# Attention slots taken two at a time, with the softmax denominators applied after the product with the values

## The reference

```python
q = heads(xn @ wq.T); lat = xn @ w_kv_down.T; k = heads(lat @ w_k_up.T); v = heads(lat @ w_v_up.T)   # 16 heads of 64
q, k = rope(q), rope(k)
probs = softmax(q @ k.T / 8 + causal)
s = (probs @ v, heads joined) @ wo.T
e_star = max(top-2 experts of xn @ gate_w + gate_b)
g = silu(2 * (gelu(xn @ w1[e_star] + b1[e_star]) @ w2[e_star] + b2[e_star]))
out = x + s * g
```

## Time and profile before

| | |
|---|---|
| median of 3 runs | 309.83 us (309.74 to 309.87) |
| the profiled execution | 310.5 us, span 308.7 us |
| PE / DVE / ACT / POOL busy | 294.3 / 221.0 / 242.9 / 215.9 us |
| granted TensorE clock | 0.998 |
| chain that ended last | PE 64%, POOL 12%, issue 11%, DVE 8%, ACT 2% |

### The profile page before, as it was taken

One profiled execution on the slowest core, in us unless ns is written; L12 is line 12 of the kernel. 1 busy time (PEld: TensorE's weight loads), 2 busy tenths in 40 slices (PEclk: granted clock), 3 DMA queues, 4 the chain that ended last, 5 costly groups with the idle time before them and its releaser, 6 DMA issues.

```text
span 308.7 us, 8487 instructions
## 1 busy us (share of the span) xinstructions
PE 294.3 (95%) x2362; PEld 235.4 (76%) x2362; DVE 221.0 (72%) x883; ACT 242.9 (79%) x851; POOL 215.9 (70%) x321
## 2 busy tenths in 40 slices
PE   8897999999999999999999989999989999899994
PEld 3566878888888888777777789999867777786763
DVE  3889998987787998988887523323278789898651
ACT  3387889898887889999897665555799999889982
POOL 3378878786786879999999933332138999889730
PEclk9999999999999999999999999999999999999999
DMA  6764595979333333333345470000063334344200
GB/s 204 232 140 112 107 308 124 225 168 302 74 69 71 68 71 89 92 87 87 99 104 134 129 197 0 2 2 0 3 187 71 93 102 115 103 108 133 71 19 17
DMA packets 39596, 33.35 MB, mean 108 GB/s; under 512 B 4801, under 2 KB 36674, under 8 KB 39554
## 3 DMA queue, kind: packets, MB, share of 16 engines
q1 hardware_dynamic: 38098, 30.51, 38.3%
q0 software_dynamic: 1024, 2.10, 2.5%
q10 hardware_dynamic: 432, 0.23, 0.3%
HBM read 11.07 MB, written 4.98 MB: 52 GB/s over the span
## 4 chain that ended last, share of the span: by engine, by line
PE 64%; POOL 12%; issue 11%; DVE 8%; ACT 2%; DMA 1%; POOLq 1%; SPq 0%; DVEq 0%; ACTq 0%
PE bank L1092 9%; PE bank L1080 8%; PE bank L1106 7%; PE bank L1120 6%; PE bank L1285 6%; PE bank L1300 6%; POOL probs L474 5%; POOL staged L463 4%; PE bank L1054 3%; DVE rot_out L585 3%; PE bank L1108 3%; PE bank L1082 3%; DVE masked L594 2%; PE bank L1188 2%; PE bank L1070 2%
## 5 line engine op out<-in xcount | busy, mean ns | idle before, releaser
L885 ACT ACTIVATE pexp<-masked,negmax 128x128 f32<-128x128 f32 (+1 forms) x256 | 114.1, 452 | 1.5 <-DVE negmax L594 1.4
L474 POOL TENSOR_SCALAR probs<-pexp,rden 128x256 f32<-128x256 f32 (+1 forms) x184 | 80.3, 451 | 26.0 <-DVE rden L601 23.3
L594 DVE CUSTOM_DVE_ANT_0 masked<-bank,mask 128x128 f32<-128x128 f32 (+1 forms) x256 | 75.9, 351 | 27.1 <-PE bank L1082 26.9
L463 POOL TENSOR_TENSOR staged<-rot_out 128x512 f32<-128x512 f32 x63 | 80.2, 1275 | 17.8 <-DVE rot_out L585 17.3
L585 DVE TENSOR_TENSOR rot_out<-bank,rot 128x1024 f32<-128x1024 f32 x64 | 77.6, 1214 | 4.0 <-PE bank L1056 2.7
L907 ACT COPY probsT<-bank 128x384 f32<-128x384 f32 x128 | 54.9, 480 | 22.9 <-PE bank L1092 21.9
L1092 PE MATMUL bank<-ident,probs 128*128 128x128 f32 x384 | 54.7, 275 | 1.8 <-ACT probsT L907 0.9
L885 ACT ACTIVATION_READ_ACCUMULATOR pexp<-masked,negmax 128x1 f32 x256 | 49.9, 195 | 0.0
L1080 PE MATMUL bank<-qk_sb 64*128 64x256 f32 x256 | 45.0, 427 | 2.9 <-DVE negmax L594 2.1
L1092 PEld LDWEIGHTS bank<-ident,probs 128*128 128x128 f32 x384 | 43.1, 140 | 5.2 <-POOL probs L474 1.9
L1120 PE MATMUL bank<-vo_sb,ctxT 128*128 128x128 f32 x256 | 39.4, 278 | 0.7 <-ACT ctxT L914 0.7
(11 more groups left out here) (113 smaller groups left out, 458.1 us busy)
## 6 DMA issues: line engine op xcount, KB each, us to landing
qk_sb<-staged SPq DMA_DIRECT2D x128, 128.0 KB, 2.5
w_sb<-in_w SPq DMA_DIRECT2D x2, 1024.0 KB, 5.6
w_sb<-in_w SPq DMA_DIRECT2D x4, 512.0 KB, 4.9
sorted_x<-z SPq DMA_DIRECT2D x1, 1408.0 KB, 7.9
sorted_g<-z SPq DMA_DIRECT2D x1, 1152.0 KB, 5.5
out<-res SPq DMA_DIRECT2D x8, 128.0 KB, 1.8
x_sb<-in_x SPq DMA_DIRECT2D x3, 256.0 KB, 3.8
rot<-in_c_rot SPq DMA_DIRECT2D x1, 512.0 KB, 5.0
```

What stands on the lines that cost most here:

```text
L463: pool.tensor_tensor(staged[:, n % 2, :, m % 2, :], rot_out[:, m % 2, :, 0:S], rot_out[:, m % 2, :, S:2 * S], op=ALU.add).then_inc(staged_ ...
L474: pool.tensor_scalar(probs[:, g % 2, i, c], pexp[:, g % 2, i, c], rden[:, g % 2, i, k:k + 1], 1.0, ALU.mult, ALU.mult).then_inc(probs_read ...
L594: t = dve.tensor_tensor_reduce(masked[:, g % 2, i, c], s_bank[i][:, c], mask[:, c], -1.0, -NEG * 1e8, ALU.add, ALU.min, negmax[:, g % 2, i ...
L885: e = act.activation(pexp[:, g % 2, i, c], masked[:, g % 2, i, c], ACT.Exp, bias=negmax[:, g % 2, i, k:k + 1], scale=-1.0, accum_out=rowsu ...
```

## The change

From slot 24 on (`FIRST_DOUBLE`) each engine takes two slots at a time (`couple(g)`, g even). The exponentials are transposed as they are, without `scale`. The eight reciprocals of a token row (two slots, two heads, two row halves) are transposed by PE to eight rows, copied by ACT to `rden_rows`, written to DRAM by one transfer and read back by two that spread them over 64 partitions each (`shares`); `ctx_out`, now on DVE, multiplies the result of `values` by them. Only slots 38, 39, 62 and 63 are still scaled first, by DVE and POOL, in place. `scores_of_two` puts the rests of two slots side by side in `s_bank` and their corners in `t_bank`; DVE must have read the corners before `turn` may write there. PE's order in a couple is: scores of the next two slots, outputs g-4 and g-3, a projection, `turn(g)`, a projection, `turn(g+1)`, values of g-2 and g-1. `TWICE` moves from (36, 38) to (23, 25). No slot from 24 on stands in `ALONE`.

```diff
-TWICE = (36, 38)
+TWICE = (23, 25)
...
-ALONE = tuple(range(FIRST_DOUBLE)) + (G_LEAD - 2, G_LEAD - 1, B * NP - 2, B * NP - 1)
+ALONE = tuple(range(FIRST_DOUBLE))
...
+def coupled(g):
+    return g >= FIRST_DOUBLE
...
+def scaled(g):
+    return g < FIRST_DOUBLE or g in (G_LEAD - 2, G_LEAD - 1, LAST, LAST + 1)
...
+def units(u):
+    return [n for n in range(UNIT, u + 1) if not scaled(2 * n)]
...
-        rden = sb("rden", [P, 2, 2, 2])
+        rden = sb("rden", [P, 2, 2, 2, 2])
...
+        def corner(g, i):
+            if g % 4 < 2 or not coupled(g - 2):
+                return masked[:, g % 2, i, 0:P]
+            return more_corners[:, g % 2, i, :]
...
+        def v_bank(g):
+            return s_bank[1] if g == G_LEAD - 2 else o_bank
...
+            def rows_out(u):
+                sp.wait_ge(row_ready, len(units(u)))
+                sp.dma_start(share_rows[u].rearrange("n i k p -> (n i k) p"), rden_rows[u % 2]).then_inc(row_out, 16)
+            def rows_back(u):
+                sp.wait_ge(row_out, 16 * len(units(u)))
+                if u < UNIT + 2:
+                    sp.wait_ge(probsT_done, 2 * FIRST_DOUBLE)
+                else:
+                    sp.wait_ge(ctx_ready, values_through(2 * u - 4))
+                for i in range(2):
+                    sp.dma_start(shares[HD * i:HD * i + HD, u % 2],
+                                 share_rows[u, :, i].rearrange("n k p -> n (k p)").unsqueeze(0)
+                                 .broadcast_to([HD, 2, S])).then_inc(row_in[u % 2], 16)
...
+            def couple(g):
+                if g == G_LEAD - 2:
+                    sp.wait_ge(scattered, 16 * NT)
+                    load(0, 4, xs_in)
+                if not scaled(g):
+                    rows_out(g // 2)
+                    rows_back(g // 2)
+                for m in (*items(g), *items(g + 1)):
+                    if m % 2:
+                        place(m // 2)
+                if g == G_LEAD - 2:
+                    load(4, NR, xs_rest)
+                for n in (g, g + 1):
+                    if n in FINALS:
+                        store(FINAL_ORDER.index(FINALS[n]))
             def finish(b):
...
+            def couple(g):
+                if scaled(g + 1):
+                    scale(g + 1)
+                for n in range(g, g + 2):
+                    for m in items(n):
+                        rotated(m)
+                    if SCATTER_SLOT <= n < SCATTER_SLOT + NT:
+                        scatter(n - SCATTER_SLOT)
+                    if GATHER_SLOT <= n < GATHER_SLOT + NT:
+                        gather(GATHER_ORDER[n - GATHER_SLOT])
+                if g < LAST and scaled(g + 2):
+                    scale(g + 2)
...
+            def corner_max(g):
+                dve.wait_ge(scores_done, g + 1)
+                dve.wait_ge(exp_done, 2 * g - 6)
+                for i in range(2):
+                    t = dve.tensor_tensor_reduce(corner(g, i), t_bank[i][:, g % 2 * P:(g % 2 + 1) * P], mask[:, 0:P],
+                                                 -1.0, -NEG * 1e8, ALU.add, ALU.min, negmax[:, g % 4, i, 0:1])
+                t.then_inc(corner_read, 1)
+            def rest_max(g):
+                dve.wait_ge(exp_done, 2 * g - 2)
+                for i in range(2):
+                    dve.tensor_tensor_reduce(masked[:, g % 2, i, P:SW], s_bank[i][:, g % 2 * S:(g % 2 + 1) * S], mask[:, P:SW],
+                                             -1.0, -NEG * 1e8, ALU.add, ALU.min,
+                                             negmax[:, g % 4, i, 1:2]).then_inc(masked_ready, 1)
...
+            def ctx_out(g):
+                u = g // 2
+                dve.wait_ge(pv_done, values_through(g))
+                dve.wait_ge(y_step, g + 2 - NP)
+                o, heads = v_bank(g)[:, 0:2 * S], ctxT[:, g % NP:g % NP + 2, :].rearrange("p n s -> p (n s)")
+                if scaled(g):
+                    dve.tensor_copy(heads, o).then_inc(ctx_ready, 1)
+                else:
+                    dve.wait_ge(row_in[u % 2], 32 * sum(n % 2 == u % 2 for n in units(u)))
+                    dve.tensor_tensor(heads, o, shares[:, u % 2].rearrange("p n s -> p (n s)"),
+                                      op=ALU.mult).then_inc(ctx_ready, 1)
+            def couple(g):
+                if g - 4 >= FIRST_DOUBLE and g not in (G_LEAD, G_LEAD + 2):
+                    ctx_out(g - 4)
+                if g < LAST:
+                    corner_max(g + 2)
+                    corner_max(g + 3)
+                denominators(g + 1)
+                if scaled(g + 1):
+                    scale(g + 1)
+                if g < LAST:
+                    rest_max(g + 2)
+                for m in items(g):
+                    rotate(m)
+                if (g + 1) // NP < LEAD and (g + 1) % NP == 3:
+                    take_y((g + 1) // NP - 1)
+                if FINALS.get(g + 1, -1) >= LEAD:
+                    finalise(FINALS[g + 1])
+                if g < LAST:
+                    rest_max(g + 3)
+                    denominators(g + 2)
+                if g < LAST and scaled(g + 2):
+                    scale(g + 2)
+                for n in range(g, g + 2):
+                    if FINALS.get(n, LEAD) < LEAD:
+                        finalise(FINALS[n])
+                if g in (G_LEAD - 2, LAST):
+                    ctx_out(g - 2)
+                for m in items(g + 1):
+                    rotate(m)
             def finish(b):
+                ctx_out(NP * b + NP - 2)
...
             def exponentials(g, i):
                 act.wait_ge(masked_ready, 2 * g + i + 1)
+                if g >= FIRST_DOUBLE + 2:
+                    act.wait_ge(probsT_done, 2 * g + i - 3)
+                    act.wait_ge(rden_ready, g - 1)
                 for k, c in enumerate(rows):
...
                     act.wait_ge(pv_done, values_through(g - 4))
                 for i in range(2):
                     act.wait_ge(probsT_done, 2 * g + i + 1)
+                    if i and g % 2 == 0 and not scaled(g):
+                        u = g // 2
+                        wait(act, row_out, 16 * (len(units(u)) - 2))
+                        act.copy(rden_rows[u % 2], t_bank[1][0:8, SW:SW + P]).then_inc(row_ready, 1)
                     act.copy(probsT[:, g % 4, i, :], t_bank[i][:, 0:SW]).then_inc(probsT_ready, 1)
...
+            def couple(g):
+                if g == FIRST_DOUBLE:
+                    exponentials(g + 1, 0)
                     ctx_out(g - 2)
-                if g == G_LEAD:
-                    exponentials(g + 1, 0)
-                ctx_out(g - 1)
-                if g == G_LEAD:
                     exponentials(g + 1, 1)
-                    scale(g + 1)
+                turned_probs(g)
+                if g < LAST:
+                    exponentials(g + 2, 0)
+                    if g != G_LEAD - 2:
+                        exponentials(g + 2, 1)
+                turned_probs(g + 1)
+                if g == G_LEAD - 2:
+                    exponentials(g + 2, 1)
+                if g < LAST:
+                    for i in range(2):
+                        exponentials(g + 3, i)
+                if g == FIRST_DOUBLE:
+                    ctx_out(g - 1)
...
+            def scores_of_two(g):
+                pe.wait_ge(masked_ready, 2 * g)
+                for n in range(2):
+                    p = (g + n) % NP
+                    pe.wait_ge(qk_in[p], 32 * (g // NP) + 32)
+                    for i, r in enumerate(half_rows):
+                        pe.matmul(s_bank[i][:, n * S:(n + 1) * S], qk_sb[r, 0, p, P:S], qk_sb[r, 1, p, :], start=True, stop=True)
+                pe.wait_ge(probsT_ready, 2 * (g - 2))
+                for n in range(2):
+                    p = (g + n) % NP
+                    for i, r in enumerate(half_rows):
+                        m = pe.matmul(t_bank[i][:, n * P:(n + 1) * P], qk_sb[r, 0, p, 0:P], qk_sb[r, 1, p, 0:P],
+                                      start=True, stop=True)
+                m.then_inc(scores_done, 2)
             def turn(g):
+                wait(pe, corner_read, corners_through(g + 3 - g % 2))
                 for i in range(2):
                     wait(pe, probsT_ready, 2 * g + i - 1)
+                    if not scaled(g):
+                        pe.wait_ge(exp_done, 2 * g + i + 1)
+                    if i and g % 2 == 0 and not scaled(g):
+                        pe.wait_ge(rden_ready, g + 2)
+                        pe.transpose(t_bank[1][0:8, SW:SW + P], rden[:, g // 2 % 2].rearrange("p n i k -> p (n i k)"), ident[:])
                     for k in range(3):
-                        if k < 2:
-                            pe.wait_ge(probs_ready[i][k], g + 1)
-                        t = pe.transpose(t_bank[i][:, k * P:(k + 1) * P], probs[:, g % 2, i, k * P:(k + 1) * P], ident[:])
+                        if k < 2 and scaled(g):
+                            pe.wait_ge(probs_ready[i][k], scaled_through(g))
```

(52 more changed lines are left out.)

139 lines of the change are left out of this document (58 added, 81 removed).

## The result

The changed kernel took 324.52 us (median of 4 runs, 322.75 to 326.19), the kernel before 309.85 beside it: a ratio of 1.047 (95% interval 1.041 to 1.053), 14.7 us slower. The prediction had slower, but 319.5, with a range to 323. The profiled execution has a span of 322.0 us, 13.3 more than before, at a mean granted clock of 0.986.

What follows compares the result with a forecast made beforehand. PE, dense in the middle, bounded the kernel before; a four-engine chain of 7.24 us a couple would then set the pace over PE's 6.8. Stages summed to +10.1 us, 319.9, stated as 319.5; range 311 to 323.

Steps and rivals of the forecast that it cites:

- Experts: the same list: 0: Expert phase between couple 38 and slot 40: instruction list unchanged, so 0 us later.
- the chain that the prediction named: From one `turn` to the next couple's, over four engines: 7.24 us a couple, +0.31 over 6.93; chance 0.60.
- `finalise`: Sequences 0, 1 and 2, in couples 48, 52 and 54, stand on DVE's chain: 0.96 us each, in full.
- 44 to 55: Couples 44 to 54: six at 7.24 plus three `finalise` at 0.96, 46.3 against 42.42 us, +3.9.
- 40 to 43: Slots behind the experts: two couples of 5.8 us from `turn` to `turn`, 13.7 against 13.08 us, +0.7.
- from 56: Last couples to the end: 32.9 to 33.1 us against 30.27, +2.8.
- Slots 28 to 37: Couples 28 to 36: five couples at +0.31 us each, +1.6.
- The rows: Spread reciprocals: DRAM round trip of 6.3 us, wanted by `ctx_out` at 11.9 us, 5.6 us of cover, so free.
- 1 (PE sets the pace): Middle couples: chain has slack, 7.0 or less, PE sets the pace at 6.9; +5.7, 315.5 us; chance 0.20.
- 4: Whole kernel: no change that can be told, gains and new waits even, 309.8 us; chance 0.04.
- 3: Reciprocals' round trip not covered, SP behind a `store` or slow transfers, each couple waits; 340 us; chance 0.03.
- 2, the faster one: Without `scale` POOL's gaps go, PE's list is 0.1 to 0.15 us a couple shorter; 305 us; chance 0.13.

Runs made afterwards that it cites:

- e1: The change with the load of the later sorted_x tiles issued right behind the first four tiles, not behind `place`: 320.57 us, 1.030 of the kernel before.
- e3: The change with DVE's `ctx_out` of slots g-2 and g-1 ahead of the second rotation, at the end of couple g: 321.75 us, ratio 1.031.
- e5: The change with the edits of e1 and e3 together: 315.73 us, 1.018 of the kernel before.
- e6: e5 with DVE's `finalise` of the early sequences moved ahead of `rest_max(g+3)`: 314.60 us, 1.012 of the kernel before.
- e9: e6 with POOL's `scale(38)` ahead of couple 36's last add and scatter: 316.48 us, 1.013 of the kernel before.
- e13: e10 with reciprocals' rows ahead of `place` in SP's queue, each couple's `place` one couple later, only from couple 26 on: 312.88 us, ratio 1.007.
- e10: e9 with DVE's `ctx_out(60)` ahead of `scale(62)`: 316.32 us, 1.011 of the kernel before.
- e7: e6 with ACT in couple 40 copying slot 41's transposes ahead of the exponentials of slot 42: 315.19 us, 1.016 of the kernel before.
- e8: e7 without spreading the reciprocals, `ctx_out` a plain copy, so those slots lack their denominators: 314.44 us, 1.014 of the kernel before.
- e4: The kernel before with only the load of the later sorted_x tiles moved behind `place` of slot 39: 316.59 us, 1.017 of the kernel before.

## Why the direction was right and the size was not

- **The step that failed** is "Experts: the same list: 0". The list of PE is the same, but SP's is not: the load of tiles 4 and on was moved behind `place`, which waits for POOL. It cost 5.2 us of the 13.3, of which 3.84 are the wait and the rest the clock behind it. The rest adds to 8.1, where 10.1 were forecast. The prediction did look at SP's queue for the rows, and did not walk it for the one transfer that the diff moves; the row that prices it, two loads gone by 173.8 before, was in the trace. With this step alone mended (e1) the change takes 320.57 us, inside the forecast's 311 to 323.
- **The direction** held without that step: e1 is still at 1.030. But the chain that the prediction named makes only 1.4 us of the rest (11 couples at 0.13 over 6.93) and `finalise` behind it 2.7; the others lie at both ends and behind the experts. Stages forecast too high (24 to 37, 44 to 55) and too low (38, 40 to 43, from 56) partly cancel, so that 8.1 came near 10.1 is in part luck.
- **The chain of the couple** was right in every link up to `ctx_out`: copies from 0.58 (forecast 0.58), exponentials from 1.49 (1.50), reciprocal 3.39 (3.39), `ctx_out` 4.61 (4.61), its end 5.29 (5.29). The joint and two outputs took 0.97 instead of 1.14, and the projection 0.80 instead of 0.81, so 7.06 instead of 7.24. Eight records of the same kind follow at one pace, and the 0.10 added for longer records was not there. e3 shows that this chain sets the pace and that PE's own is 6.78.
- **Slots 28 to 37**: forecast +1.6, measured −0.3. The chain's size is 0.8 of it; the other 1.0 is nearly all a plain omission: couple 36 had a third projection before (7.84 us against 6.93), and the change moved it to slots 23 and 25.
- **`finalise`**: forecast 3 x 0.96, all before slot 56. Couples 50 and 54 paid 1.02 and 0.78; the third falls into the stretch from 56, whose first couple took 7.12 where the second took 6.24. The price was right, 2.7 in all, and its place half wrong, which makes 44 to 55 too long and the end too short.
- **40 to 43**: forecast +0.7, measured +1.7, and the difference is clock. PE's second half of the scores waits 1.90 us for ACT's copy of slot 41, behind the table load and the exponentials of slot 42. e5 and e6 have the same wait, and their clock stays at 1.00; the change, e1 to e3 and e9 to e13 have it, and the clock falls (0.68 and 0.50 in the change's windows 237:239 and 239:241). The three rows are PE's after that wait in the change, e9 and e5, and the windows e9's and e5's behind it:

```profile
237.40 0.97 PE L1236 MATMUL bank<-qk_sb 64*128 64x128 f32 x8 [1.90 <-ACT probsT L1051]
```

```profile
231.36 1.23 PE L1234 MATMUL bank<-qk_sb 64*128 64x128 f32 x8 [1.90 <-ACT probsT L1049]
```

```profile
231.12 0.72 PE L1234 MATMUL bank<-qk_sb 64*128 64x128 f32 x8 [1.90 <-ACT probsT L1049]
```

```profile
231.00:233.00 2.00, 1.64 (x10) 1.42 (x11) 1.27 (x4) 2.00 (x9) 1.01 (x1) 0.58 0.19 53
```

```profile
232.00:234.00 2.00, 1.87 (x16) 1.65 (x16) 1.95 (x14) 1.32 (x6) 1.03 (x1) 1.00 0.21 57
```

  Couple 42 takes 8.40 us in e5 and 9.59 in e9. Without the fall (e5) the stretch is 13.59 us, +0.5, so the walk to +0.7 was right, and the 1.2 is the clock's.
- **The rows**: forecast 5.6 us of cover, measured 3.6 in one couple, and 2.2 to 4.5 in the eight others whose landing is in the trace. From `turn` at 247.54 the row's copy ends at 248.8, SP sends it at 249.1, it is back in the queue at 251.25, the second way leaves by 252.5 and lands, by the median of 3.1 us, at 255.6, for the `ctx_out` at 259.21. That was enough in the profile of the change, and not with `ctx_out` 1.13 us earlier and couples 0.28 shorter: besides e9 and e10, e3 waits 0.96 us for the rows once, and e5, e6 and e7 0.24, 1.35 and 0.56 us in couple 60. The fit in the Trainium skill ("DMA: Bandwidth & Descriptors", Anatomy of one DMA) is for transfers that GpSimd issues, and the prediction used it for SP's. By it 128 KB would take an estimated 2.3 us; the way back took 3.1, so the measurement stands.
- **The rivals**: 1 (PE sets the pace) and 4 are out, 3 is out for the change. 2, the faster one, had a true core: PE's shorter list is worth 0.15 us a couple once the chain is out of its way (6.78 against 6.93), and the six edits of e13 bring 3.9 of the 4.7% back. POOL is at 55% busy, not 40.
- The product of PSUM and SBUF took 0.675 to 0.692 us in all 18 records, as estimated from 128 and 1024 columns. POOL's adds, which ran beside 13 of them, never lengthened it; so says the Trainium skill for one input in PSUM ("SBUF — State Buffer", SBUF: two separate sides), and the trace agrees.

What stays open is why the same wait of 1.90 us brings the lower clock in some executions and not in others. It is not a matter of the kernel alone: of e5's six executions two had a mean clock of 1.00 and took 314.04 and 314.90 us, the other four 0.991 to 0.995 and 315.72 to 316.31; e7's four divide likewise, while all six of e13 stayed at or under 0.994. Only one execution of each kernel has a trace, so where the others lost their clock is not shown. Nor was it tried why couple 38's stretch grew by 0.6 us where 0.1 was walked.

## What to carry to other kernels

Walk every engine's queue for each transfer that a diff moves, SP's first: what is the instruction now ahead of it waiting for, and who reads what the transfer brings. A block can be priced at "the same list" only if all five lists are the same. And count the clock behind a stall: 3.8 us of idle PE cost 5.2.

When work is moved in pairs, the latency chain through four engines, not the busiest one's work, can set the pace, as it did here; take the step that isn't needed (here one rotation) out of it before counting the saving. Most cures showed a next wait that had been hidden behind the last one, so the cover of a transfer has to be counted anew at the faster pace.

## What the runs showed of the hardware

- After PE had stood still for 3.84 us (DMA at 0.94 of its engines), the granted clock was 0.51 for some 3 us of dense matmuls, then 1.00. Behind a wait of 1.90 us it fell to 0.5 in the change, e1 to e3 and e9 to e13, and stayed at 1.00 in e5 and e6. Behind one of 1.70 us (couple 38) it fell in e3, e6 and e8 and not in e5 and e7; behind one of 3.0 to 3.1 us (couple 42) it fell in e8 and not in e7. In e4, where PE had been idle for 3.89 us at the same place, the mean over the experts was again 0.97; in e1, without the stall, 1.00.
- A transfer of 4 KB into DRAM, and SP's wait for it, took 2.0 to 2.4 us in 11 of the change's 18 couples and 2.7 to 3.8 in five, with the same code around it. A cover of some 2 us (3.6 less the 1.1 of the rotation and the shorter couples) fails at such a couple, not on the mean: for e9's row of 140.83 it took 3.3 us, behind 2.3 in SP's queue.
- The copy of 8 x 128 from PSUM on ACT took 0.26 us beside 0.48 for 128 x 384: 0.16 between starts, so it cost the chain less than its own record shows.
